# Cross-attention layers of a 12-layer decoder: maxima's scores of two heads laid into the two row halves of the array

## What is computed

```python
def _L1_xattn_ref(query_states, key_value_states, Wq, bq, Wk, bk, Wv, bv, Wo, bo):
    NUM_HEADS = 16
    HEAD_DIM = 128 // NUM_HEADS          # 8
    q = query_states @ Wq.T + bq         # 256 tokens
    k = key_value_states @ Wk.T + bk     # 512 keys
    v = key_value_states @ Wv.T + bv
    ...
    scores = jnp.einsum('bhqd,bhkd->bhqk', q * SCALE, k)
    attn = jax.nn.softmax(scores, axis=-1)
    ctx = jnp.einsum('bhqk,bhkd->bhqd', attn, v)
    return ctx @ Wo.T + bo
x = x + _L1_xattn_ref(_layernorm(x, axis=-1), ctx_1024, ...)
```

## Time and profile before

| | us |
|---|---|
| median of 3 runs (2597.37 to 2599.72) | 2599.3 |
| the profiled execution's own time | 2597.72 |
| its span, first to last instruction | 2595.9 |
| mean granted TensorE clock, share of 2.4 GHz | 0.933 |
| PE busy, share of the span | 88% |
| DVE, ACT, POOL busy | 60%, 50%, 28% |

### The profile page before, as it was taken

How to read it: one execution, slowest core, us unless ns; L and a number is a source line. 1 busy time by engine, 2 the same in 40 slices (tenths; PEclk the granted TensorE clock), 3 DMA queues, 4 the chain that set the end, 5 groups by cost and what they waited for, 6 DMA issues and landing times. The chain is left out here.

```text
span 2595.9 us, 48375 instructions
## 1 busy us (share of the span) xinstructions
PE 2275.9 (88%) x16585; PEld 1478.1 (57%) x16585; DVE 1563.2 (60%) x4614; ACT 1306.7 (50%) x3591; POOL 722.2 (28%) x996
## 2 busy tenths in 40 slices
PE   8879997789898599976889998887779999899989
PEld 5635544755555245543756766566747776466643
DVE  5667762246666778745366664553366775877730
ACT  5646661235556166652356676422235565466632
POOL 2232202444432522200633231234421121322100
PEclk8989998879999699997989999988989999899999
DMA  2123316220000133220600000265410001232100
GB/s 80 31 71 102 97 41 199 46 65 34 18 34 17 50 100 105 83 84 29 157 3 2 1 1 15 84 137 147 135 37 2 10 2 40 84 86 80 52 19 17
DMA packets 127203, 155.40 MB, mean 60 GB/s; under 512 B 22496, under 2 KB 90345, under 8 KB 125810
## 3 DMA queue, kind: packets, MB, share of 16 engines
q1 hardware_dynamic: 116850, 143.20, 19.3%
q0 software_dynamic: 7488, 7.78, 1.4%
q10 hardware_dynamic: 2624, 1.32, 0.3%
HBM read 117.96 MB, written 34.99 MB: 59 GB/s over the span
## 5 line engine op out<-in xcount | busy, mean ns | idle before, releaser
L540 ACT ACTIVATE L3x_p_ring<-L3x_ps_t 128x512 f32<-128x512 f32 x256 | 141.7, 599 | 101.2 <-PE L3x_ps_t L615 100.1
L442 DVE CUSTOM_DVE_ANT_0 L3x_ps_s<-L3x_ps_s,L3x_mask_q 128x512 f32<-128x512 f32 x256 | 170.1, 718 | 27.6 <-PE L3x_ps_s L596 26.3
L540 ACT ACTIVATE L1x_p_ring<-L1x_ps_t 128x512 f32<-128x512 f32 x256 | 138.0, 623 | 76.9 <-PE L1x_ps_t L613 76.8
L540 ACT ACTIVATE L0x_p_ring<-L0x_ps_t 128x512 f32<-128x512 f32 x256 | 138.0, 626 | 72.7 <-PE L0x_ps_t L613 72.6
L445 DVE TENSOR_REDUCE L0x_mx<-L0x_ps_s 128x2 f32<-128x1024 f32 x128 | 151.9, 1221 | 29.4 <-PE L0x_ps_s L596 29.0
L445 DVE TENSOR_REDUCE L1x_mx<-L1x_ps_s 128x2 f32<-128x1024 f32 x128 | 152.1, 1221 | 21.6 <-PE L1x_ps_s L596 20.4
L1087 ACT ACTIVATE L2a_probs<-L2a_ps_s,L2a_top 128x256 f32<-128x256 f32 x256 | 117.8, 472 | 78.6 <-DVE L2a_top L1022 78.5
L1087 ACT ACTIVATE L3a_probs<-L3a_ps_s,L3a_top 128x128 f32<-128x128 f32 (+1 forms) x256 | 104.0, 422 | 40.1 <-DVE L3a_top L1018 37.9
L613 PE MATMUL L3x_ps_t<-L3x_q_stack,L3x_k_stack 128*128 128x256 bf16 x512 | 120.3, 274 | 1.7 <-DMA L3x_q_stack<-L3x_m_rows 1.4
L615 PE MATMUL L3x_ps_t<-L3x_mask_k,const_ident_bf 128*128 128x256 bf16 x512 | 119.9, 274 | 0.0
L596 PE MATMUL L1x_ps_s<-L1x_k_stack,L1x_q_stack 125*128 125x512 bf16 x256 | 80.6, 397 | 16.3 <-PEq L98 11.8
(11 more groups left out here) (769 smaller groups left out, 6056.0 us busy)
## 6 DMA issues: line engine op xcount, KB each, us to landing
L2f_w_e<-L2f_in_w_e SPq DMA_DIRECT2D x23, 544.0 KB, 3.7
L0f_w<-L0f_in_w SPq DMA_DIRECT2D x32, 256.0 KB, 6.9
L1a_rk_wide<-L1a_rk_dram SPq DMA_DIRECT2D x8, 1024.0 KB
L1f_w<-L1f_in_w SPq DMA_DIRECT2D x32, 256.0 KB, 3.4
L0x_k_stack<-L0x_k_dram SPq DMA_DIRECT2D x84, 96.0 KB
L1x_k_stack<-L1x_k_dram SPq DMA_DIRECT2D x84, 96.0 KB
L3x_k_stack<-L3x_k_dram SPq DMA_DIRECT2D x84, 96.0 KB
kept_x<-ctxT SPq DMA_DIRECT2D x24, 256.0 KB, 3.2
```

The costliest lines, as they stand in the source:

```text
L442: last = dve.tensor_tensor_reduce(span, span, mask_q[:, t, :], 1.0, 2 * MASKED, ALU.add, ALU.max, accum_out=mx[:, t, k:k + 1])
L540: act.activation(p_ring[:, u % RING, j * BANK:(j + 1) * BANK], t_bank(o), ACT.Exp, scale=scale).then_inc(out["t"].sem, 1)
```

## The change

The stacks get another layout by the head's parity. For an even head the q and k parts are in rows 0 to 71 (of which `s` reads rows 0 to 63) and its maxima in rows 125 to 127; for an odd head the parts are in rows 56 to 127 (of which `s` reads rows 64 to 127) and its maxima in rows 0 to 2. Rows 0 to 63, and 64 to 127, hold all part products but the smallest or all of them. So `s` now takes two heads at a time and one half of the queries: one matmul in rows 0 to 63 for the even head and one in rows 64 to 127 for the odd head, into two PSUM banks. The number of matmuls, reductions and slots is the same. `t` still reads all 128 rows.

Since the heads of a quarter are now in two row layouts, each stack quarter takes 6 DMAs for k and 6 for q, of two heads each, where it took 3 and 3 of four heads. The maxima take 6 DMAs of four heads a half, where it took 3 of eight. The store of k gains a fourth slot in DRAM and a second DMA. The prologues change in the same way.

```diff
+Q_SLOTS = (0, 1, 2, 0, 1)
+K_SLOTS = (2, 0, 1, 2)
+STACK_ROWS = (((0, 1, 1), (24, 2, 1), (48, 0, 1)), ((56, 2, 0), (80, 0, 0), (104, 1, 0)))
+MAX_ROWS = (P - 3, 0)
+def store_parts(eng, name, dram, parts, stored):
+    if name == "q":
+        eng.dma_start(dram[0:3].rearrange("i p k -> p i k"), parts[:]).then_inc(stored, 16)
+        eng.dma_start(dram[3:5].rearrange("i p k -> p i k"), parts[:, 0:2, :]).then_inc(stored, 16)
+    else:
+        eng.dma_start(dram[1:4].rearrange("i p k -> p i k"), parts[:]).then_inc(stored, 16)
+        eng.dma_start(dram[0:1].rearrange("i p k -> p i k"), parts[:, 2:3, :]).then_inc(stored, 16)
+def load_quarter(eng, name, stack, dram, par, quarter, stacked):
+    for odd in range(2):
+        heads = slice(QUARTER * quarter + odd, QUARTER * (quarter + 1), 2)
+        for row, q_slot, k_slot in STACK_ROWS[odd]:
+            slot = q_slot if name == "q" else k_slot
+            eng.dma_start(stack[row:row + 24, par, heads], dram[slot:slot + 3].rearrange("i (d h) k -> (i d) h k", h=16)[:, heads]
+                          ).then_inc(stacked, 16)
...
-                        heads = slice(HALF * k, HALF * (k + 1))
                         wait_out(sp, ("m", k, b))
-                        for i in range(3):
-                            sp.dma_start(q_stack[MAX_ROW + i:MAX_ROW + i + 1, par, heads],
-                                         m_rows[H * i + HALF * k:H * i + HALF * (k + 1), k]).then_inc(m_stacked[k].sem, 16)
+                        for odd in range(2):
+                            for i in range(3):
+                                sp.dma_start(q_stack[MAX_ROWS[odd] + i:MAX_ROWS[odd] + i + 1, par, HALF * k + odd:HALF * (k + 1):2],
+                                             m_rows[H * i + HALF * k + odd:H * i + HALF * (k + 1):2, k]).then_inc(m_stacked[k].sem, 16)
...
-                            last = dve.tensor_reduce(mx[:, :, k], s_bank(o), AX, ALU.max)
+                            last = dve.tensor_reduce(mx[:, t, 2 * u:2 * u + 2], s_bank(o), AX, ALU.max)
...
-                        for t in range(QT):
-                            last = pe.matmul(s_bank(o)[:, t, :], q_stack[0:MAX_ROW, par, k, t * P:(t + 1) * P], k_stack[0:MAX_ROW, par, k, :],
+                        u, t = k // 2, k % 2
+                        for j in range(2):
+                            rows, h = slice(j * P // 2, (j + 1) * P // 2), 2 * u + j
+                            last = pe.matmul(s_bank(o)[:, j, :], q_stack[rows, par, h, t * P:(t + 1) * P], k_stack[rows, par, h, :],
                                              start=True, stop=True)
...
-                    rows = prologue.stacks[name][P // 2:P, par].rearrange("p h k -> p (h k)").bitcast(F32)
+                    rows = prologue.stacks[name][:, par].rearrange("p h k -> p (h k)").bitcast(F32)
```

More of the change, by code:

```diff
@@ L290, in attention_cross @@
         q_split, k_split = tally("q_split", 4), tally("k_split", 4)
-        q_stored, k_stored = tally("q_stored", 32), tally("k_stored", 16)
-        m_stacked = [tally(f"m_stacked_{j}_", 3 * 16) for j in range(2)]
-        stacked = [tally(f"stacked_{j}_", 6 * 16) for j in range(H // QUARTER)]
+        q_stored, k_stored = tally("q_stored", 32), tally("k_stored", 32)
+        m_stacked = [tally(f"m_stacked_{j}_", 6 * 16) for j in range(2)]
+        stacked = [tally(f"stacked_{j}_", 12 * 16) for j in range(H // QUARTER)]
         m_steps = tally("m_steps", 8)
@@ L329, in load_stack @@
         def load_stack(eng, name, quarter, b):
[L331 to L337, removed]
+            stack, dram, stored = (q_stack, q_dram, q_stored) if name == "q" else (k_stack, k_dram, k_stored)
+            wait_tally(eng, stored, b, 32)
+            load_quarter(eng, name, stack, dram, b % 2, quarter, stacked[quarter].sem)
         with nc.Block() as block:
@@ L591, in _ @@
                         if k % QUARTER == 0 and b == 0:
-                            pe.wait_ge(prologue.stacked[k // QUARTER], 6 * 16)
+                            pe.wait_ge(prologue.stacked[k // QUARTER], 12 * 16)
                         elif k % QUARTER == 0:
-                            wait_tally(pe, stacked[k // QUARTER], b, 6 * 16)
-                        for t in range(QT):
-                            last = pe.matmul(s_bank(o)[:, t, :], q_stack[0:MAX_ROW, par, k, t * P:(t + 1) * P], k_stack[0:MAX_ROW, par, k, :],
+                            wait_tally(pe, stacked[k // QUARTER], b, 12 * 16)
+                        u, t = k // 2, k % 2
+                        for j in range(2):
+                            rows, h = slice(j * P // 2, (j + 1) * P // 2), 2 * u + j
+                            last = pe.matmul(s_bank(o)[:, j, :], q_stack[rows, par, h, t * P:(t + 1) * P], k_stack[rows, par, h, :],
                                              start=True, stop=True)
@@ L657, in __init__ @@
         self.q_dram = nc.dram_tensor(name + "first_q_dram", [5, P, S], BF16)
-        self.k_dram = nc.dram_tensor(name + "first_k_dram", [3, P, KX], BF16)
+        self.k_dram = nc.dram_tensor(name + "first_k_dram", [4, P, KX], BF16)
         self.masks = masks
     def load_stack(self, eng, name, quarter):
[L662 to L667, removed]
+        load_quarter(eng, name, self.stacks[name], self.q_dram if name == "q" else self.k_dram, 0, quarter, self.stacked[quarter])
 def attention_rows(nc, x_sb, const, w, cfg, ahead, follow, stacks, opening, prologue):
@@ L3614, in fill @@
                 def fill(name, par):
-                    rows = prologue.stacks[name][P // 2:P, par].rearrange("p h k -> p (h k)").bitcast(F32)
+                    rows = prologue.stacks[name][:, par].rearrange("p h k -> p (h k)").bitcast(F32)
                     words = two_ones if name == "k" else const["zero"]
-                    act.activation(rows, words[P // 2:P, 0:1].broadcast_to(list(rows.shape)), ACT.Copy).then_inc(filled, 1)
+                    act.activation(rows, words[:, 0:1].broadcast_to(list(rows.shape)), ACT.Copy).then_inc(filled, 1)
                 act.wait_ge(two_made, 1)
```

28 lines of the change are left out of this document (12 added, 16 removed).

## The result

The changed kernel takes 2765.55 us (median of 4 runs, 2763.28 to 2768.88), against 2599.51 for the kernel before on the same chip: a ratio of 1.064, 95% interval 1.062 to 1.066. The forecast was 2752. The profiled execution is 2763.4 us with a span of 2761.6, 165.7 us more than the span of before.

What follows compares the result with a forecast made beforehand. PE looked the bound before, SP and POOL after. Complete rounds add 46 + 46 + 23, seventh rounds 14, first maxima 9, last halves 11, L1x's start 5: 154 on 2597.7, 2752 us; own range 2690 to 2810, 8-in-10 range 2635 to 2850.

Steps and rivals of the forecast that it cites:

- The loop: In the cross layers, SP's issues, POOL's splits and the landing of k's store set the round: 36.9 us.
- Price of a load: On SP, issues keep their price at half the bytes: 0.41 us a stack load, 0.69 a load of maxima.
- Rivals 2 and 4: 2: two-head stack loads issue in 0.2 us, 2642 us, chance 0.08; 4: two-dimensional loads cost 0.5, about 2900, 0.08.
- rival 3: SP's extra issues are covered, only the array counts: 2592 us, or 2516 with free shape changes; chance 0.08.
- Rounds alike: Sign of being right: rounds of 37 us in all three layers, L0x, L1x and L3x, alike.
- The sum: Extra time over L0x, L1x and L3x rounds, layer edges and the start of L1x: 154 us, giving 2752.
- The first stacks of L1x: Twelve more q loads ahead of L1x, with PE idle until SP is through: 4.9 us more.
- The array: Pairs save 0.21 us a step, tile-shape changes cost 0.19; 0.24 us a batch is left, under 6 us.
- Rival 1: On PE, pairs of `s` don't run at once: 76 us more, 2828 us; chance 0.06.
- The 82 us that I gave for free changes: On PE, were tile-shape changes free, 384 steps would save 0.21 us each, 82 us: 2516 us.
- No slack at `t`: In L0x and L1x the half-0 maxima's landing, 1.28 us after their issue, releases `t`; 0.7 us slack in L3x.
- Seventh round: Each layer's last round has no stores, so PE sets it: 34.7 us, 36.0 in L3x; 14 us in all.

Runs made afterwards that it cites:

- e1: Kernel before, one head at a time, with only the change's doubled stack and maxima loads and two stores of k: 2757.28 us, ratio 1.063.
- e4: The whole change plus one idle POOL instruction ahead of its split of k in batches 1 to 7: 2800.5 us in one run.
- e11: The whole change with half-0 maxima ahead of the next batch's stack quarter 0 in SP's order: 2839.1 us in one run.
- e12: e6 with half-0 maxima ahead of the next batch's stack quarter 0 in SP's order: 2584.49 us, ratio 0.994.
- e13: Kernel before, one head at a time, with merged loads (outermost count 24) and half-0 maxima ahead of stack quarter 0: 2586.67 us, ratio 0.996.
- e8: e6 with both heads' scores read from rows 0 to 63, so pairs can't run at once: 2651.7 us in one run.
- e10: Kernel before with only its maxima loads doubled, stacks untouched: 2640.7 us in one run.
- e6: The change with merged loads, 4 a stack quarter and 2 a maxima half, rows reordered so the outermost dimension counts 24: 2602.55 us, ratio 1.0025.

## Why the prediction was right, step by step

- **The loop.** Its links in the round shown above, measured against the forecast: maxima 3.8 (4.1); three quarters and the context 17.1 (15.2); landing of the last load to POOL 1.6 (2.2); split of q 2.8 (2.8); of k 4.6 (4.7); k's store 0.9 (0.4, only the second issue was in it); its landing 2.1 (2.6); quarter 0 4.9 (4.9): 37.7 against 36.9. The links are those named, and in that order; e1 and e4 show that the loads make the loop and that POOL is in it. The largest miss, 1.9, is for the most part one load that took 1.75 us to issue. Of all 1008 stack loads 30 took over 0.45 us and 13 of them over 1 us; before it was 12 and 5 of 504. What holds them up stayed open.
- **Price of a load.** 0.41 us for a stack load of two heads: right (371 ns and the gap, in 168 of each kind). Maxima 0.615, not 0.69: 573 ns for half as many pieces, 642 before. Rivals 2 and 4 fall with that, and rival 3 with the time itself.
- **Rounds alike.** Mean of six: 37.0 in L0x, 37.2 in L1x, 37.8 in L3x. L3x's extra lies in k's store, which landed after 3.8 us in two of seven batches; it had done so in two before (4.0).
- **The sum.** L0x grew by 60.4 us (58 in the forecast), L1x by 62.3 (58), L3x by 37.5 (31), 160.2 against 148. The first stacks of L1x cost what was forecast: PE is idle for 16.75 us ahead of its first score where it had been 11.79. But between the end of L0x and that score only 0.9 us were added, because the first 47 us of L1a, which the change doesn't touch, ran at a higher clock in this execution and took 4.4 us less (the two windows at the end). 2.9 us more lie between L1x and L3x, 1.5 at the start. Neither the 4.4 nor the 2.9 belongs to the change: e4 and e11, with the same code in these places, show 47.1 and 42.7 us in L1a, and both have 4 us less than the change between L1x and L3x. So that the total came within 0.5% of the forecast is in part luck: misses of both signs met in it, in the links above and here.
- **The array.** The two changes of shape take what a pair saves: a step of 0.86 us against 0.87, and what is left is 0.24, 0.24 and 0.19 us a batch in e12 against e13, where I had 0.24. The pair's two matmuls start 0.003 us apart (within 0.01 in the forecast). Rival 1 falls by e8. The 82 us that I gave for free changes were probably too many, by e8.
- **No slack at `t`.** Right in the main by e10: 1.6 us more of issues ahead of half 0 is 1.55 us of wait in the shown rounds, half 1 untouched, and 1.3 us of round.
- **Seventh round.** 36.7, 34.5 and 34.8 us; the forecast had 34.7, 34.7 and 36.0.

## What to carry to other kernels

Count the issues of a queue before the cycles of the array: a change that saves work on PE by cutting each load in two pays for it in the queue that issues the loads, and where a store's landing and a split on another engine close the loop, it pays the whole excess each round. When loads are merged to save issues, look at the outermost dimension that is left: here it decided between loads that kept 3 of 16 DMA engines busy, the last of them landing 9.2 us behind its issue, and loads that landed in time. And moving a transfer forward in a queue's order helps only if its data are ready by then; otherwise it is a wait with the queue behind it.

## What the hardware showed beyond that

After the longer of PE's two waits the granted clock fell. Windows of the changed kernel, columns as above:

```profile
280.50:283.10 2.60, 0.12 (x3) 0.03 (x2) 1.65 (x2) 0.98 (x3) 0.00 (x0) 1.00 0.03 5
299.00:304.00 5.00, 0.02 (x1) 0.03 (x1) 0.20 (x1) 0.60 (x1) 3.14 (x5) 0.82 0.05 15
304.00:306.00 2.00, 2.00 (x9) 0.97 (x10) 0.40 (x1) 1.08 (x2) 1.84 (x3) 0.50 0.61 168
306.00:309.00 3.00, 3.00 (x19) 1.33 (x21) 2.05 (x2) 2.39 (x5) 1.92 (x2) 0.50 0.04 10
309.00:312.00 3.00, 3.00 (x42) 1.53 (x32) 0.74 (x2) 0.24 (x2) 0.00 (x0) 1.00 0.51 172
```

PE idled for 2.5 us in the first stretch and kept its upper level; it idled for 5.0 in the second, and then ran at the lower one (0.50, 1.2 GHz) until 309, so the first `t` took 1.01 us instead of 0.60. In L0x the mean clock is 0.88. I had no term for it. SP and POOL set the round here, so it cost little; where PE bounds the time, the 5 us at half the clock behind such a pause would cost some 2.5 us of PE's work, by my estimate from these rows. The clock also differs between executions. Here are the first 47 us of L1a, the same work in each, in the profile of before and then in that of the change:

```profile
520.80:568.00 47.20, 40.74 (x165) 23.03 (x166) 22.37 (x68) 16.13 (x34) 27.57 (x29) 0.72 0.23 67
```

```profile
583.80:626.60 42.80, 33.69 (x162) 19.60 (x165) 21.77 (x66) 16.09 (x33) 25.74 (x24) 0.86 0.25 74
```

A difference of a few us between two traces can come from such a stretch alone; in the fourteen traces this one takes 42.7 to 51.6 us, at a mean clock of 0.86 to 0.60.

The issue of a stack load went by its number of rows and not by its bytes: 364 ns (median) for 24 rows of 4 KB and the same for 24 of 2 KB, 371 for 24 rows of two pieces, about 760 for 72 rows of 1 or 2 KB (e6).
